# A fused attention and mixture-of-experts block on one core: rows of the stacked operand interleaved six partitions apart, and the first batch row's head slots reordered

## The reference

```python
ct_q = _lin(x, w_down_q, b_down_q)
q = (_lin(ct_q, w_up_q, b_up_q) + _rope(_lin(ct_q, wq_r, bq_r), cos, sin)).reshape(bs, sl, nh, hd)
ct_kv = _lin(x, w_down_kv, b_down_kv)
k = (_lin(ct_kv, w_up_k, b_up_k) + _rope(_lin(ct_kv, wk_r, bk_r), cos, sin)).reshape(bs, sl, nh, hd)
v = _lin(ct_kv, w_up_v, b_up_v).reshape(bs, sl, nh, hd)
scores = jnp.einsum('bqhd,bkhd->bhqk', q, k) / np.sqrt(hd)
probs = jax.nn.softmax(scores, axis=-1)
a = jnp.einsum('bhqk,bkhd->bqhd', probs, v).reshape(bs, sl, nh * hd)
x = x + _layernorm(_lin(a, wo, bo))
x = x + _layernorm(_L0_ffn_ref(_layernorm(x), ...))
```

## Time and profile before

| | us |
|---|---|
| median of 3 runs | 431.63 (431.09 to 433.25) |
| profiled execution, its own time | 429.76 |
| its span, first to last instruction | 427.9 |
| TensorE busy | 397.9 (93% of the span) |
| VectorE / ScalarE / GpSimd busy | 273.4 / 208.1 / 129.6 |
| mean granted TensorE clock | 0.985 of full speed |

### The profile page before, as it was taken

How to read it: one execution, slowest core, us unless ns; L and a number is a source line. 1 busy time by engine, 2 the same in 40 slices (tenths; PEclk the granted TensorE clock), 3 DMA queues, 4 the chain that set the end, 5 groups by cost and what they waited for, 6 DMA issues and landing times.

```text
span 427.9 us, 9422 instructions
## 1 busy us (share of the span) xinstructions
PE 397.9 (93%) x3383; PEld 299.3 (70%) x3383; DVE 273.4 (64%) x629; ACT 208.1 (49%) x383; POOL 129.6 (30%) x184
## 2 busy tenths in 40 slices
PE   7998789999999999797989999999999999999990
PEld 6675456676776767374668999999994444589990
DVE  5674478787879786877475594222225898727775
ACT  1644647676675858555561112444446766311110
POOL 1423412516253434303211101212212220026872
PEclk9999899999999999899999999999999999999997
DMA  8899326364553736460127660011111111123422
GB/s 263 204 116 122 62 70 194 87 175 136 153 156 89 216 96 209 100 199 1 52 98 230 223 215 25 26 51 51 50 51 44 44 45 35 51 59 104 141 95 86
DMA packets 50756, 47.29 MB, mean 111 GB/s; under 512 B 5334, under 2 KB 45526, under 8 KB 50710
## 3 DMA queue, kind: packets, MB, share of 16 engines
q1 hardware_dynamic: 44779, 38.31, 34.2%
q0 software_dynamic: 1632, 4.46, 3.6%
q10 hardware_dynamic: 4299, 3.92, 2.7%
HBM read 25.19 MB, written 8.65 MB: 79 GB/s over the span
## 4 chain that ended last, share of the span: by engine, by line
PE 79%; DVE 8%; DMA 4%; issue 3%; ACT 3%; POOL 2%; ACTq 0%; DVEq 0%; POOLq 0%
PE bank L1388 40%; PE bank L1707 7%; PE bank L1392 6%; PE bank L1576 6%; PE bank L1556 5%; PE bank L1517 5%; PE bank L1732 3%; DMA stacks<-mT 2%; PE bank L1455 2%; DVE nmax L1057 2%; PE bank L1445 2%; PE bank L1503 1%; DVE wall L1087 1%; DVE stats_at L991 1%; POOL rstd_at L641 1%
## 5 line engine op out<-in xcount | busy, mean ns | idle before, releaser
L1057 DVE TENSOR_REDUCE nmax<-bank 128x2 f32<-128x512 f32 x112 | 74.4, 686 | 26.4 <-PE bank L1517 25.6
L1388 PEld LDWEIGHTS bank<-stacks,wall 128*128 128x128 f32 x512 | 59.8, 192 | 2.5 <-issue 1.9
L1388 PE MATMUL bank<-stacks,wall 128*128 128x128 f32 x512 | 61.2, 276 | 0.4 <-ACT stacks L909 0.4
L1263 DVE TENSOR_TENSOR stacks<-stacks,bank 128x512 f32<-128x512 f32 x34 | 23.3, 687 | 51.7 <-PE bank L1388 49.1
L873 ACT ACTIVATE pv<-bank 128x512 f32<-128x512 f32 x64 | 38.3, 603 | 36.7 <-PE bank L1576 35.8
L1576 PE MATMUL bank<-stacks 99*128 99x256 bf16 x256 | 49.5, 276 | 3.8 <-DMA stacks<-mT 3.3
L873 ACT ACTIVATE wall<-bank 128x512 f32<-128x512 f32 x64 | 38.5, 606 | 27.2 <-PE bank L1576 26.2
L909 ACT ACTIVATE stacks<-bank 128x512 f32<-128x512 f32 x34 | 20.3, 597 | 64.3 <-PE bank L1388 54.3
L1517 PE MATMUL bank<-stacks 96*128 96x256 bf16 x224 | 43.2, 278 | 6.4 <-DVE nmax L1057 6.2
L1388 PE MATMUL bank<-wall,stacks 128*128 128x256 f32 (+1 forms) x208 | 49.2, 380 | 0.0
L706 POOL DMA_INDIRECT stacks<-x_sc,row_i x18 | 19.9, 1105 | 89.5 <-PE bank L1392 70.5
(11 more groups left out here) (207 smaller groups left out, 795.4 us busy)
## 6 DMA issues: line engine op xcount, KB each, us to landing
stacks<-low_sb SPq DMA_DIRECT2D x144, 64.0 KB, 2.5
wall<-gate_up SPq DMA_DIRECT2D x8, 1024.0 KB, 5.4
wall<-down SPq DMA_DIRECT2D x8, 512.0 KB, 6.9
y_exp<-stacks ACTq DMA_DIRECT2D x18, 128.0 KB, 1.7
x_tok<-wall SPq DMA_DIRECT2D x8, 256.0 KB, 2.5
stacks<-x_tok SPq DMA_DIRECT2D x16, 128.0 KB, 2.5
out<-stacks SPq DMA_DIRECT2D x8, 256.0 KB, 2.1
stacks<-low_sb SPq DMA_DIRECT2D x12, 128.0 KB, 5.9
```

The source lines that it names most:

```text
L1057: dve.tensor_reduce(nmax[:, half, qt, 2 * pair:2 * pair + 2], two(sm_bank[u % 2]), AX.X, ALU.max, negate=True).then_inc(sm["sm_max"], 1)
L1263: dve.tensor_tensor(to, sg, fu[:, :], ALU.mult).then_inc(sm["h_sb"], 1)
L1388: last = pe.matmul(out_ap, lhsT, rhs, start=(n == 0), stop=(n == len(pairs) - 1))
```

## The change

It does five things.
1. The DMAs that fill the 96 rows of `stacks` write the pair r into the partitions r, r+6, r+12, ..., r+90 instead of 16r to 16r+15. Their number, size and order stay. The three rows 96 to 98 stay.
2. ct of batch row 2 and then S15 move from behind head 0 to the end of the prologue, ahead of head 0.
3. In slot 0, M1 moves from behind head 5 to behind head 3, and GpSimd's part of it now stands ahead of the variance power of row 3; the evictions move from behind head 5 to behind head 4; M0 from behind head 14 to behind head 13. M1's DMA was on ScalarE's queue and is there still.
4. The 16 SM steps of row 1 stand behind heads 8 to 15, two each.
5. The two evictions of q of batch row 2 go from ScalarE (L822) to VectorE, ahead of the first SM maximum. TensorE gets 12 more matmuls on ones at the start (66 instead of 54) and two times eight more, behind the first transposes and behind the first ct.

```diff
-WARM_ONES = 54
+WARM_ONES = 66
...
-        MOVED = {"A_R": 2, "A_T": 2, "A_Q": 3, "A_QK": 4, "M1": 5, "A_ev0": 5, "A_ev1": 5,
+        MOVED = {"A_R": 2, "A_T": 2, "M1": 3, "A_Q": 3, "A_QK": 4, "A_ev0": 4, "A_ev1": 4,
                  "A_khigh": 6, "A_qhigh": 7, "N_v": 8,
-                 "M0": 14}
+                 "M0": 13}
...
-        PROLOGUE = ((0, "O_rows W_ones B_stats B_power B_norm B_xnT"),
+        PROLOGUE = ((0, "O_rows W_ones B_stats B_power B_norm B_xnT W_few"),
                     (1, "B_stats B_power B_norm"),
-                    (0, "A_ones B_ct"),
+                    (0, "A_ones B_ct W_few"),
...
-                    (0, "S12 S13 S14"))
-        FIRST_ROW = {0: ((2, "B_ct B_ct1"),)}
+                    (0, "S12 S13 S14"),
+                    (2, "B_ct B_ct1"),
+                    (0, "S15"))
...
-            if h < 9:
-                return () if h else ((0, NH - 1),)
-            u = 2 * (h - 9) + (h == NH - 1)
-            return tuple((1, n) for n in range(u, u + 2 + (h >= NH - 2)))
+            if h < 8:
+                return ()
+            return tuple((1, n) for n in range(2 * (h - 8), 2 * (h - 8) + 2))
...
-                                    stacks[HD * r:HD * r + HD, b, side, :, :].rearrange("d h c -> d (h c)"),
+                                    stacks[r:ROWS:NSLOT, b, side, :, :].rearrange("d h c -> d (h c)"),
...
-                                        half_of(stacks[HD * r:HD * r + HD, b % 2, side, :, :], m),
+                                        half_of(stacks[r:ROWS:NSLOT, b % 2, side, :, :], m),
...
-            order = {0: ("M1",), 2: ("B_power",), 8: ("A_kres", "M0",),
+            order = {0: ("P_M1",), 2: ("B_power",), 8: ("A_kres", "M0",),
...
-                    act.activation(qf[:, m, :], two(w1)[:, m, :], ACT.Identity, bias=bcol[:, 2 + m:3 + m]
-                                   ).then_inc(sm["q_sb"], 1)
+                    if b != 2:
+                        act.activation(qf[:, m, :], two(w1)[:, m, :], ACT.Identity, bias=bcol[:, 2 + m:3 + m]
+                                       ).then_inc(sm["q_sb"], 1)
...
+            def third_q(m):
+
+                def f(b, par):
+                    if b != 2:
+                        return
+                    dve.wait_ge(sm["qk_ps"], 3)
+                    dve.wait_ge(sm["ql"], 2)
+                    dve.wait_ge(sm["q_sb"], 4)
+                    dve.tensor_scalar(qf[:, m, :], two(w1)[:, m, :], bcol[:, 2 + m:3 + m], None, ALU.add
+                                      ).then_inc(sm["q_sb"], 1)
+                return f
```

More of the change, by code:

```diff
@@ L315, in program @@
         block = ctx.enter_context(nc.Block())
-        MOVED = {"A_R": 2, "A_T": 2, "A_Q": 3, "A_QK": 4, "M1": 5, "A_ev0": 5, "A_ev1": 5,
+        MOVED = {"A_R": 2, "A_T": 2, "M1": 3, "A_Q": 3, "A_QK": 4, "A_ev0": 4, "A_ev1": 4,
                  "A_khigh": 6, "A_qhigh": 7, "N_v": 8,
-                 "M0": 14}
-        AHEAD = {"B": 3, "A": 2, "N": 1, "M0": 1, "M1": 0, "C": 0, "D": -1, "E": -2}
-        PROLOGUE = ((0, "O_rows W_ones B_stats B_power B_norm B_xnT"),
+                 "M0": 13}
+        AHEAD = {"B": 3, "A": 2, "N": 1, "M0": 1, "M1": 0, "P": 0, "C": 0, "D": -1, "E": -2}
+        PROLOGUE = ((0, "O_rows W_ones B_stats B_power B_norm B_xnT W_few"),
                     (1, "B_stats B_power B_norm"),
-                    (0, "A_ones B_ct"),
+                    (0, "A_ones B_ct W_few"),
                     (1, "B_xnT"),
@@ L396, in run_slot @@
                         step_of(steps, name, b, par)
[L397 to L400, removed]
                 for name in MOVED:
@@ L677, in _ @@
             steps = {
-                "M0": lambda b, par: m_split(b, par, 0), "P_M0": lambda b, par: m_split(b, par, 0), "M1": lambda b, par: m_split(b, par, 1),
+                "M0": lambda b, par: m_split(b, par, 0), "P_M0": lambda b, par: m_split(b, par, 0), "P_M1": lambda b, par: m_split(b, par, 1),
                 "B_power": lambda b, par: power("in", b + 1, rstd["in"][:, :], var["in"][:, :], TB),
@@ L711, in _ @@
             steps["L"] = routed_tile
-            last = {0: "M1:7", 1: "E_score:0 D_power:6 D_x1:6 D_power2:6"}
+            last = {0: "P_M1:7", 1: "E_score:0 D_power:6 D_x1:6 D_power2:6"}
             run_attention(pool, nothing, steps, order, last)
@@ L1113, in _ @@
             steps = {
-                "O_rows": ones, "A_ones": ones_and_sums, "A_kv": keys_sum, "A_T": rope,
+                "O_rows": ones, "A_ones": ones_and_sums, "A_kv": keys_sum, "A_T": rope, "A_ev0": third_q(0), "A_ev1": third_q(1),
                 "H_k0": first_k(0), "H_k1": first_k(1), "B_stats": a_stats, "B_norm": a_norm, "N_v": v_add, "SM": sm_max,
@@ L1396, in warm_bf, with ones_on @@
                 pe.wait_ge(sm["setup_dve"], 1)
-                for _ in range(WARM_ONES):
+                ones_on(WARM_ONES)
+            def ones_on(n):
+                for _ in range(n):
                     pe.matmul(w2[:, 0:P], ones_bf[:, :], ones_bf[:, :], start=True, stop=True)
@@ L1643, in d_router @@
                 last.then_inc(sm["rt_ps"], 1)
-            steps = {"W_ones": warm_bf, "H_Q": first_qk_a, "H_QK": first_qk_b,
+            steps = {"W_ones": warm_bf, "W_few": lambda b, par: ones_on(8), "H_Q": first_qk_a, "H_QK": first_qk_b,
                      "B_xnT": a_xnT, "B_turn": a_xnT, "B_ct": a_ct, "B_ct1": lambda b, par: ct_half(b, 1), "A_R": a_rope, "A_Q": a_q,
```

## The result

The kernel before took 432.50 us and the changed one 427.77 us (medians of six runs each, 424.66 to 428.77 for the changed one); the ratio is 0.989, with a 95% interval of 0.986 to 0.993. That is faster by 1.1%, 4.7 us in the medians, where 5.1 was forecast; the forecast 426.5 is 1.3 us low. The profiled execution took 428.47 us, with a span of 426.6, only 1.3 us less than the 427.9 of the one before. So the medians agree with the forecast sum, and the two traces don't seem to. Why they differ is the question of this study.

The account below looks back on a forecast made before the run. TensorE's own work was taken as the bound from slot 1 on, so only slot 0 and the prologue could gain: 1.1 + 1.7 + 2.3 = 5.1 us, from 431.6 to 426.5 us, range 424.8 to 430.2.

Parts of the forecast that it names:

- ct and S15 ahead of head 0: Start of slot 0: this work covers the wait for the first maxima; head 1 comes 1.1 us earlier.
- M1 earlier: Slot 0: second maxima's DMA issued about 38.9 instead of 43.01; head 8 at 43.4, a term of 1.7 us.
- q's evictions on VectorE, cost nothing: Slot 0, about 40.8 us: two instructions of some 0.5 us fit VectorE's idle time; up to 1.0 us if not.
- Rival 2: Slot 0: the clock drops in the new 1.0 us hole before head 7; gain 3.5 us, time 428.1; chance 0.12.
- SM two per head, and the walk to slot 1: Slot 0 from head 8: with row 1's stacks there, slot 1 starts at 56.4 instead of 61.48 us.
- The interleaved rows: Slot 0: rows six apart lift row 1's stacks above 118 GB/s, so they land in time for SM steps at 43.65.
- rival 1: Slot 0: interleaving moves nothing, TensorE waits for the stacks behind head 8; gain 1.6 us, time 430.0; chance 0.14.
- Matmuls on ones, cost 0: Prologue: the added matmuls fill TensorE's idle holes; cost 0, or 0.5 us if the cover were gone; no gain counted.
- All that was won stays won: Slots 1 to 7: order kept, TensorE's holes some 0.3 us a slot, so the gain of slot 0 remains.
- Rivals 3 and 4: First: distant rows slow later slots' transfers, 442 us, chance 0.04; second: maxima still land last, 428.6 us, chance 0.05.

Follow-up runs that it names:

- experiment 5: The changed kernel run again, unchanged; 426.63 us, ratio 0.986 to the kernel before.
- experiment 2: The kernel before with only the stacks rows placed six partitions apart; 427.53 us, ratio 0.989.
- experiment 1: The changed kernel with each piece's 16 rows next to each other again; 431.58 us, ratio 0.998.
- experiment 10: The changed kernel with neighbouring rows throughout and each transfer of the first two rows cut in two of 8 rows; 442.77 us, one run.
- 7: The changed kernel with the two q evictions of row 2 back on ScalarE; 428.96 us, ratio 0.991.
- 12: The changed kernel with row 2's q evictions back on ScalarE and 24 matmuls on ones in TensorE's wait before head 7; 427.07 us, ratio 0.987.
- 9: The changed kernel with rows two apart inside a block of 32 partitions instead of six apart; 427.36 us, one run.
- experiment 3: The changed kernel with 12 and 16 matmuls on ones in TensorE's two waits ending slots 5 and 6; 424.63 us, ratio 0.982.
- 6: The changed kernel with 54 ones at the start, no groups of eight, and 12 and 16 in the waits ending slots 5 and 6; 423.52 us, ratio 0.979.
- experiment 4: The changed kernel with 54 matmuls on ones instead of 66 and without the two groups of eight; 424.55 us, ratio 0.985.

## Why the prediction was right, and where it wasn't

*ct and S15 ahead of head 0*: right in the times. Heads 0 and 1 start back to back from 35.65 (35.35 and 35.6 forecast); 0.2 of that stood in the profile from the first transposes on, and in experiment 5 the two start at 35.48. No run moves these two alone, and experiment 2 shows that the layout takes the wait before head 0 away by itself, so this term is not the reordering's alone.

*M1 earlier*: right, but its price rested on a row that holds only where few transfers are still in front. "With the 3.17 us of the old one" is true of a DMA issued at 43.01, when the engines were busy with the stacks for only 1.4 us more; issued at 40.06, in the middle of them, it took 7.76 (experiment 1), and in experiment 10, issued at 48.30, some 8. Head 8 came at 43.95 against 43.4, 0.2 of the 0.55 being the late start, and the hole before head 7 is 0.89 against 1.0.

*q's evictions on VectorE, cost nothing*: right, and undersold. I took ScalarE as it would be, and never priced what it would be without the move: 0.7 us, and 1.7 more by the clock (7, 12). Rival 2, the clock falling behind a hole before head 7, is what happens at 1.61 us and did not happen at 0.89.

*SM two per head, and the walk to slot 1*: from head 8 to slot 1 13.0 us forecast and 13.03 measured; the clock stayed at 1.00. Slot 0 gained 4.5 instead of 5.1.

*The interleaved rows*: right in the mechanism and in the landing times, 2.4 to 2.9 us against 2.5 forecast (1, 2, 9). The port count in it was off by one for two of the six pairs (14, not 13), on which nothing hangs. Wrong was the split between this term (2.3) and the others (1.1 and 1.7), and with it rival 1: without the layout I gave the change 1.6, and experiment 1 shows no gain, because the early DMA depends on it too. There TensorE stood for the maxima (2.91 us) and not, as rival 1 has it, for the stacks. The terms were not independent.

*Matmuls on ones, cost 0*: this term failed. In slot 0 it is 0; in the combine, 370 us later, all ten traces with them are 1.3 to 2.3 us longer than the four without, and between 5 and 4, and 3 and 6, nothing else differs. I looked for the cost only where the ones stand.

*"All that was won stays won"*: of the 4.5 us, 1.2 were lost to the clock in the profiled execution and 2.0 in the combine. Where the clock did not fall, the slots kept their length: 318.5 to 318.7 us to the mark in experiments 1, 3, 6, 10 and 12, and 320.25 in the kernel before, with one fall. That the forecast still came within 1.3 us is partly luck: two costs that I had at nothing, the falls behind the waits and the combine, stand against a gain that I had not counted. The profile I started from was a good execution of the kernel before (mean clock 0.985, where the median of the 17 was 0.978), so its median held more time at low clock than I saw, and the change takes away a wait behind which the clock fell.

*Rivals 3 and 4* did not happen: in later slots the 64 KB transfers land in 2.0 us instead of 2.5, and head 8 came 2.3 earlier.

**Open.** What makes the combine longer. Timeline of DVE, experiment 4:

```profile
389.73 0.42 DVE L1367 TENSOR_TENSOR stacks<-bank,pv 128x256 f32<-128x256 f32 x1 [0.69 <-DMA out<-stacks]
390.07 0.42 DVE L1367 TENSOR_TENSOR stacks<-stacks,pv 128x256 f32<-128x256 f32 x1
```

Timeline of DVE, experiment 5:

```profile
390.20 0.42 DVE L1367 TENSOR_TENSOR stacks<-bank,pv 128x256 f32<-128x256 f32 x1 [1.22 <-DMA out<-stacks]
390.54 1.85 DVE L1367 TENSOR_TENSOR stacks<-stacks,pv 128x256 f32<-128x256 f32 x1
```

The landing of one `out` write, which VectorE waits for, comes some 0.5 us later, and the instruction after it stretches to 1.85 us. In experiment 3 the time is lost elsewhere, at the start of the combine, so this is not the whole of it. Why ones at the start do this was not tried, and other counts than 54 and 66 were not run. Why the clock fell in experiment 2 with no wait in front is open too.

## What to carry to other kernels

Look first at where a DMA's rows land: 16 neighbouring partitions held the rate at 118 GB/s here where 200 were possible, and the small transfers behind them paid too, so price a moved DMA at what the queue will be when it is issued. A wait on TensorE costs its own length, and often as much again behind it through the clock; matmuls on ones inside the wait cost nothing here (3, 6, 12), and ones elsewhere have to be measured to the end of the kernel. Cut both traces at the same few marks before explaining a total: one profiled execution here hid 3 of 4.5 us.

## What the runs showed that I had not expected

- A fall of the granted clock is a matter of chance: behind the same pair of waits (0.84 and 1.09 us) it came in 10 of 24 cases, and lasted from 3 to 7 us; in slot 0 it came behind waits of 1.61, 2.06, 2.91, 7.38 and 7.54 us, not behind 0.89, 1.18 and 1.91, and once behind no wait at all.
- 64 KB to 8 neighbouring partitions: 68 to 76 GB/s, the DMA engines' share only 0.57; to 8 rows six apart the same transfers, at 97 GB/s, need a share of 0.35, and the last landed in 2.29 us.
- A 12 KB transfer on ScalarE's queue took 7.76 us while SyncE's transfers to neighbouring partitions kept the DMA engines busy.
- Twenty-eight more matmuls of under 0.1 us each in the first 11 us of a kernel go with 1.8 us more in its last 46, in the mean of ten traces against four.
